# Mask constants fetched in pieces of 64, 24, 3 and 1 rows, and a batch's two stores issued by ACT

## The reference: what is computed

```python
x = x + xattn(layernorm(x), ctx, ctx, igate, fgate, outnorm_weight)
x = x + ffn(layernorm(x), w12, w3, gate_w)

# xattn: q, k, v as 8 heads of 32; i and f are gates per head and token
cs = cumsum(log_sigmoid(f)); log_D = cs[s] - cs[t] + i[t] for t <= s, else -inf
max_log_D = max over t; D = exp(log_D - max_log_D)
C = (q @ k.T / sqrt(32)) * D
h = (C / (max(|sum_t C|, exp(-max_log_D)) + 1e-6)) @ v      # then a layernorm per head

# ffn: the two best experts of x @ gate_w.T, softmax of their two scores as weights
y = sum_e p[e] * (silu(x @ w1[e].T) * (x @ w2[e].T)) @ w3[e].T
```

## Time and profile before

| | |
|---|---|
| median of 3 runs | 718.48 us (715.27 to 722.63) |
| the profiled execution's own time | 717.1 us |
| span in the profile | 715.4 us |
| PE busy in the span | 572.2 us (80%) |
| DVE, ACT, POOL busy | 464.7, 329.0, 306.6 us |
| gates, 60 to 107 us: PE busy, DMA share | 3.02 of 47 us, 0.30 |
| mixing, 141 to 283 us: PE busy, granted clock, DMA share | 124.06 of 142 us, 0.92, 0.60 |
| experts, 354 to 715 us: PE busy, granted clock | 349.20 of 361 us, 0.98 |

### The profile page before, as it was taken

The page is one execution under the profiler, slowest core; times in us unless marked ns, Lnnn a source line. Parts: engine busy times, 40 slices in busy tenths (PEclk is TensorE's granted clock), DMA queues, the critical chain, the costliest instruction groups (busy, mean ns, idle before and its releaser), DMA issues.

```text
span 715.4 us, 14990 instructions
## 1 busy us (share of the span) xinstructions
PE 572.2 (80%) x3608; PEld 473.6 (66%) x3609; DVE 464.7 (65%) x976; ACT 329.0 (46%) x736; POOL 306.6 (43%) x312
## 2 busy tenths in 40 slices
PE   3874009888897989522499999999999999999993
PEld 1331007777786877411288888888888888888883
DVE  4654203776867677789467667667677767667673
ACT  3444114555564656400155555555555555555551
POOL 2323021645454546300235545545545555455442
PEclk9997557998999899655599999999999999999997
DMA  8884136365556565270213233233333333333332
GB/s 275 278 293 134 47 116 183 123 192 170 181 179 196 164 207 165 89 269 2 46 31 59 48 59 52 52 60 52 52 60 52 53 60 48 56 59 47 58 46 22
DMA packets 72230, 77.52 MB, mean 108 GB/s; under 512 B 12866, under 2 KB 64202, under 8 KB 72204
## 3 DMA queue, kind: packets, MB, share of 16 engines
q1 hardware_dynamic: 56204, 50.98, 22.7%
q0 software_dynamic: 15712, 25.73, 19.5%
q10 hardware_dynamic: 288, 0.52, 0.2%
HBM read 53.99 MB, written 23.21 MB: 108 GB/s over the span
## 4 chain that ended last, share of the span: by engine, by line
issue 37%; DMA 16%; POOL 12%; SPq 11%; DVE 10%; PE 9%; ACT 3%; ACTq 0%; POOLq 0%; DVEq 0%
POOL xg L1095 8%; DMA out_rows<-ys,index 5%; DMA qbd<-qT_scratch 4%; POOL out_rows L1104 4%; SPq L418 3%; PE bank L1210 3%; DMA qT_scratch<-qt 3%; SPq L416 2%; DVE ohn L944 2%; PE dots L1192 2%; DMA qt<-in_w12T 2%; DVE ohp L943 1%; ACT x2n L638 1%; PE weighs L1179 1%; SPq L452 1%
## 5 line engine op out<-in xcount | busy, mean ns | idle before, releaser
L1104 POOL DMA_INDIRECT out_rows<-ys,index x71 | 112.9, 1590 | 155.3 <-DVE ys L996 147.0
L1002 DVE TENSOR_TENSOR w3l<-w,w3h 128x1024 fp32r<-128x1024 f32 x71 | 87.2, 1228 | 30.8 <-issue 29.9
L1095 POOL DMA_INDIRECT xg<-token_table,index x71 | 70.3, 991 | 74.9 <-DVE index L961 52.8
L673 ACT CAST w3h<-w 128x1024 fp32r x71 | 74.4, 1048 | 20.1 <-issue 20.1
L1324 PE MATMUL bank<-w3l,hth 128*128 128x256 f32 x284 | 76.5, 303 | 1.8 <-DVE w3l L1002 1.8
L1210 PE MATMUL bank<-aug,c 128*128 128x99 f32 (+2 forms) x512 | 68.3, 292 | 4.7 <-DVE c L801 4.6
L1210 PEld LDWEIGHTS bank<-aug,c 128*128 128x128 f32 x512 | 66.2, 209 | 8.0 <-DVE c L801 6.4
L1325 PE MATMUL bank<-w3h,hth 128*128 128x256 f32 x284 | 70.8, 283 | 0.0
L801 DVE SCALAR_TENSOR_TENSOR c<-dots,d 128x512 f32<-128x512 f32 x64 | 41.2, 686 | 43.8 <-PE dots L1192 43.2
L979 DVE TENSOR_TENSOR htl<-bank,hth 128x512 fp32r<-128x512 f32 x71 | 49.1, 692 | 25.3 <-ACT hth L663 25.3
L996 DVE TENSOR_SCALAR ys<-bank,pc 128x256 f32<-128x256 f32 x71 | 34.4, 484 | 46.5 <-PE bank L1328 46.5
(11 more groups left out here) (169 smaller groups left out, 1254.5 us busy)
## 6 DMA issues: line engine op xcount, KB each, us to landing
x<-in_x SPq DMA_DIRECT2D x32, 256.0 KB, 3.6
wst<-in_w12T POOLq DMA_DIRECT2D x26, 256.0 KB, 3.5
aug<-in_ctxv SPq DMA_DIRECT2D x16, 264.0 KB, 3.1
ct<-in_ctxT SPq DMA_DIRECT2D x16, 256.0 KB, 4.8
qT_scratch<-qt SPq DMA_DIRECT2D x16, 256.0 KB, 3.9
kt<-in_ctxT SPq DMA_DIRECT2D x16, 256.0 KB
qbd<-qT_scratch SPq DMA_DIRECT2D x64, 64.0 KB
out_rows<-x SPq DMA_DIRECT2D x16, 256.0 KB, 2.2
```

The source lines that it names most:

```text
L673: nc.scalar.copy(W3H[i][:], w3[:, bass.ds(e, 1)].rearrange("p a k d -> p (a k d)")).then_inc(w3h_ready, 1)
L1002: v.tensor_tensor(W3L[i][:], w3[:, bass.ds(e, 1)].rearrange("p a k d -> p (a k d)"), W3H[i][:].bitcast(F32), ALU.subtract).then_inc(w3l_re ...
L1095: q.indirect_dma_start(out=XG[x][:], out_offset=None, in_=table, in_offset=bass.IndirectOffsetOnAxis(ap=index[:, j:j + 1], axis=0)).then_i ...
L1104: q.indirect_dma_start(out=out, out_offset=bass.IndirectOffsetOnAxis(ap=index[:, j:j + 1], axis=0), in_=YS[o][:], in_offset=None, compute_ ...
```

## The change

Two edits. The constants of the mask are loaded in other pieces: `LG` in rows 0 to 3, 27 to 91 and 91 to 92, `RM` in rows 3 to 27, 27 to 91 and 91 to 92, for both buffers; that is 12 loads in place of 6, with the same bytes. And the two stores of a batch leave SP's step b (as b-3) and go to the end of ACT's step b (as b-2), behind the cast of the weight piece.

```diff
-        N_CONST, N_LATE, N_ROWS = 4, 6, 6
+        N_CONST, N_LATE, N_ROWS = 4, 6, 12
...
             for i in range(2):
-                for lo, hi in ((0, PARTS), (GROWS, MROWS)):
+                for lo, hi in ((0, PARTS), (GROWS, MROWS - 1), (MROWS - 1, MROWS)):
                     sp.dma_start(LG[i][lo:hi, :, :], lgc[lo:hi, :].rearrange("q (a s) -> q a s", a=2)
                                  ).then_inc(mask_rows, 16)
-                sp.dma_start(RM[i][PARTS:, :, :], rmc[PARTS:, :].rearrange("q (h s) -> q h s", h=NH)
-                             ).then_inc(mask_rows, 16)
+                for lo, hi in ((PARTS, GROWS), (GROWS, MROWS - 1), (MROWS - 1, MROWS)):
+                    sp.dma_start(RM[i][lo:hi, :, :], rmc[lo:hi, :].rearrange("q (h s) -> q h s", h=NH)
+                                 ).then_inc(mask_rows, 16)
...
-            def store(b, i):
-
-                sp.wait_ge(x2n_ready, b + 1)
-                sp.dma_start(out_t[b], X[i][:].rearrange("p c h d -> p c (h d)")).then_inc(x_out[i], 16)
-                sp.dma_start(table_t[b], X2N[i][:]).then_inc(row_out[i], 16)
-
...
-                if has(b, 3):
-                    store(b - 3, o)
             mixing(sp, step)
...
                 if has(b, 0):
                     high(b + B, wst[i][:], IN1 + 8 * (b - i) + 16, wst_in[i])
+                if has(b, 2):
+
+                    act.wait_ge(x2n_ready, b - 1)
+                    act.dma_start(out_t[b - 2], X[i][:].rearrange("p c h d -> p c (h d)")).then_inc(x_out[i], 16)
+                    act.dma_start(table_t[b - 2], X2N[i][:]).then_inc(row_out[i], 16)
```

## The result

The change takes 678.1 us in the median of 4 runs (676.35 to 680.75), the kernel before 718.6 (715.27 to 722.63): ratio 0.944, 95% interval 0.938 to 0.950 (every ratio below is to the kernel before, run beside it, with its 95% interval). That is faster, by 40.5 us in the medians, inside the range of 677 to 698 and 7 us under the forecast of 685. The profiled executions are 717.1 and 680.75 us (spans 715.4 and 679.0), 36.4 us apart; the one of after is the slowest of its four runs. What follows accounts for these 36.4.

The account below looks back on a forecast made before the run. It took one DMA engine at 26 GB/s to bound the gates and a ring over SP to bound mixing. From 717.1 us, 21 (gates) and 11.8 (loop) off and 1 (tail) added gave 685.3, predicted as 685, range 677 to 698.

Parts of the forecast that it names:

- The gates: Before mixing: with constants spread over engines, the store of `-M` is issued 18.7 us earlier and lands faster; gain 21 us.
- The second condition: At the gates' end: PE also waits until the first two weight pieces are split, at 81.6 to 89.4 us.
- The loop: In mixing: without the stores on SP the period falls from 11.68 to 10.7 us; gain 11.8 us over 12 batches.
- the 0.3 us for ACT's delay: In mixing: added to the 10.4 us period, as the stores delay ACT's copy 0.97 us against 0.92 of slack.
- The row against the rule: In mixing: SP's 58.4 us of waiting against the skill's rule, by which only issue time is saved, at most 8.7 us.
- The tail: After the loop: no slack in the chain of ACT's cast, copy and DVE's `wabs`; the stores add 1 us once.
- The loop gains nothing: Rival in mixing: PE and ACT become the bound, only the constants gain; 696 us, chance 0.16.
- the constants gain nothing: Rival in the gates: 64-row pieces stay on one engine or something else kept the queue; 705 us, chance 0.06.
- ACT stalls on its stores: Rival in mixing: slow issues hold ACT; 741 us at S = 5.44, chance 0.03.
- S: In mixing: what the two stores of a step cost ACT; at 2.2 us the loop gains nothing.
- More than forecast: Rival: period falls to 9.7 to 10.2 us and the landing of `-M` to its lower end; 673 to 677, chance 0.03.
- the ring of PE, DVE and ACT: In mixing: what is late next once the stores leave SP; its period lies between 9.69 and 11.68 us.

Follow-up runs that it names:

- e6_act_double: The change with each of ACT's two stores cut into two halves, so that ACT issues four: 685.6 us, ratio 0.957.
- e3_sp_order: Kernel before with the constants' new pieces and the stores (b-3) on SP behind the loads of `LG`, `RM`, `KT`, `QBD`: 778.9 us, ratio 1.085.
- e1_consts: Kernel before with only the constants in their new pieces, the stores on SP as before: 696.1 us, ratio 0.974.
- e4_sp_before_x: Kernel before with the constants' new pieces and the stores on SP, of batch b-4, ahead of the load of `X`: 682.4 us, ratio 0.951.
- e5_pool_later: The change, with POOL waiting before `w12l` until DVE has begun the step's statistics: 663.2 us, ratio 0.923.

## Why the prediction was right, and where it was off

**The gates: right, step by step.** One engine at 26 GB/s was the bound, and it went when the 89 rows were cut so that their count has divisors. Before, its work reached to 99.10 us, where the prediction had worked out 95. `kt` was expected near 71.5 and came at 72.38, because the twelve loads took 5.85 us and not 5.3 and began 0.3 us later in this execution. The store of `-M` was issued 0.9 us later than predicted, at 79.42, but took 3.1 us to SP's next issue and not 4.7, less even than the lower bound of 3.9. That the two misses nearly cancel is luck: PE started at 85.11 against the predicted 85.8. The second condition, the weight pieces, was met at 79.14 + 2.49 = 81.6 us, the early end of its bounds:

```profile
79.14 2.49 POOL L1015 TENSOR_TENSOR w12l<-qt,w12h 128x512 fp32r<-128x512 f32 x2 [4.73 <-ACT w12h L517]
```

**The loop: the mechanism right, one term mis-sized.** Predicted was 12 x (11.68 - 10.7) = 11.8 us, measured 15.7. The term is the 0.3 us for ACT's delay, 3.6 us in 12 batches, which came to nothing. The two stores cost ACT 0.92 us (191.77 to 192.69), and its copy still ended in time:

```profile
191.77 0.38 ACTq L639 DMA_DIRECT2D out_rows<-x  x1
192.31 0.38 ACTq L640 DMA_DIRECT2D token_table<-x2n  x1
193.21 0.38 ACT L591 COPY tot<-bank 128x264 f32<-128x264 f32 x1 [1.10 <-issue]
```

It ends at 193.59 and `wabs` begins at 193.69: of the slack of 0.92 0.1 is left, and from 119 to 243 us `wabs` waits for this copy not once. The period is the 10.4 that the undisturbed steps of before had shown. e6_act_double shows that the edge is there: of the next 0.9 us 0.4 come through.

**The row against the rule.** The sentence of the Trainium skill that the prediction cites ("DMA: Bandwidth & Descriptors", "Issuing engines are not separate DMA queues") speaks of the time to issue alone. By it the sum was 688, and the row, 58.4 us of waiting, was the better guide. The two runs with the stores on SP say why: in e3_sp_order SP issues in a step exactly what it issues in e1_consts, and the time goes up by 83 us; in e4_sp_before_x it issues the same again, and nearly all of the loop's gain is there. In SP's queue what counts is not the time of the issue but which loads wait behind the wait.

**The tail** was to lose 1 us, and what lies behind the first combine of batch 15 lost 0.5. The 0.5 us lost in batches 0 to 3 are in no term. So the 36.4 us are the forecast 31.8, 0.7 more from the gates, 3.9 from the loop and 0.5 from the tail, less these 0.5.

**The rivals.** "The loop gains nothing" and "the constants gain nothing" fall with the two parts apart, 17.7 and 22.6 us. "ACT stalls on its stores" needed S above 3.7 us; it was 0.92, and 0.38 for one issue. "More than forecast" had the landing of `-M` right, but its period of 9.7 to 10.2 wasn't reached, and with it not its 673 to 677.

**Named loosely in the prediction** was what is late next, "the ring of PE, DVE and ACT". The runs name it: DVE's small operations on two operands in SBUF, standing still beside POOL's `w12l`. The 10.4 us of the undisturbed steps held this stall already (0.9 to 1.6 us in each of the six), and that is why they carried over to the change; the prediction didn't know it. The best periods of before, taken as the floor (9.69), were not one: it was 9.45.

## What to carry to other kernels

When a queue stands on an ordinary load, look at the DMA share: one in sixteen pointed here at an earlier transfer that lay on one engine. A row count with divisors (64, 88) cured it; cutting the load in two didn't while one piece was still a prime (61). A store with a wait in a load queue costs what stands behind the wait, so count the batches between the wait and the loads behind it, before asking which engine issues it. And once a ring is broken, look for the next one at once: POOL's work beside DVE was worth 4 us before the change and 15 after. It showed in the trace of before already, in small operations that took six to ten times their usual time.

## What the runs showed of the hardware

- A transfer of 61 or 89 rows of 4 KB ran on one DMA engine at 26 GB/s, and the issuing queue stood for 6.56 and 12.42 us on the next load; with 64 or 88 rows no such stall came, and the counts of the semaphore fit 16 and 11 engines.
- A DVE operation of 16 elements a row with two operands in SBUF took 1.67 us beside a POOL operation of 1.28 us and ended 0.05 us after it; without POOL arithmetic beside it, 0.17. The Trainium skill ("SBUF — State Buffer", "Who interferes with whom") says that such a DVE instruction contends with a GpSimd instruction that reads SBUF, while a `tensor_reduce` never does. `mu`, a `tensor_reduce`, agrees: it took 0.67 or 0.68 us in all steps of the change, with a POOL operation beside it or not. That the stall is this port was argued from the page; that it goes when the two are pulled apart was shown. One thing stays open: `wden` began 0.34 us before `w12l` (194.63 and 194.97), twice the time that it takes undisturbed, and stood all the same.
- In e5_pool_later `w12l` starts as the second `st` ends and lies beside `mv` and the second `c`. They took 0.25 and 1.29 us for two, as in the change, where `w12l` lay elsewhere: these DVE operations did not suffer from it.
